# A decoder layer with a routed feed-forward: one flat loop of chunks on TensorE, and one chunk's code in inner loops on ScalarE and VectorE

## What is computed

```python
logits = x @ Wg.T                                     # x: 4096 x 512, normalised rows
top_v, top_i = jax.lax.top_k(logits, 2)
gates = jax.nn.softmax(top_v, axis=-1)
pos = jnp.cumsum(onehot, axis=0) - 1                  # place of a token in its expert's list
keep = pos_f < cap                                    # cap = 1280 rows per expert
exp_batches = zeros((8, cap, 512)).at[flat_e, pos_safe].set(x[tok], mode='drop')
h = jnp.einsum('ecd,edf->ecf', exp_batches, W1)       # 512 -> 2 x 1024
inp, gate = jnp.split(h, 2, axis=-1)
h = jax.nn.gelu(inp, approximate=False) * gate
exp_out = jnp.einsum('eci,eid->ecd', h, W2)           # 1024 -> 512
out = segment_sum(where(keep, gates_f, 0)[:, None] * exp_out[flat_e, pos], tok)
```

## Time and profile before

| | |
|---|---|
| median of three runs | 1554.05 us (1553.39 to 1558.0) |
| profiled execution, its own time | 1552.01 us |
| span of its instructions | 1550.3 us |
| PE busy | 1447.4 us, 93% of the span |
| DVE, ACT, POOL busy | 623.7, 568.7, 366.3 us |
| chain that ended last | PE 81%, DMA 5%, DVE 4%, "issue" 4%, POOL 3%, ACT 2% |
| the experts | from 528.64 us to the end, some 1020 us |

### The profile page before, as it was taken

One profiled execution on the slowest core, in us unless ns is written; L12 is line 12 of the kernel. 1 busy time (PEld: TensorE's weight loads), 2 busy tenths in 40 slices (PEclk: granted clock), 3 DMA queues, 4 the chain that ended last, 5 costly groups with the idle time before them and its releaser, 6 DMA issues.

```text
span 1550.3 us, 20985 instructions
## 1 busy us (share of the span) xinstructions
PE 1447.4 (93%) x7326; PEld 1214.5 (78%) x7327; DVE 623.7 (40%) x1383; ACT 568.7 (37%) x977; POOL 366.3 (24%) x354
## 2 busy tenths in 40 slices
PE   5999999999984499999999899999999999999998
PEld 4867887788772387888888788898789888897886
DVE  5634565467875243411342431215441431215211
ACT  4433433257865233312342531224431422214211
POOL 3201232137665302011112112021112112021011
PEclk9999999999996699999999999999999999999999
DMA  9100221219445426211253432026532342035112
GB/s 198 54 1 28 82 82 55 82 73 219 130 117 173 130 90 163 61 34 20 67 172 54 126 91 41 2 52 184 148 88 54 107 109 41 0 54 149 14 41 27
DMA packets 80537, 132.20 MB, mean 85 GB/s; under 512 B 31940, under 2 KB 32068, under 8 KB 79464
## 3 DMA queue, kind: packets, MB, share of 16 engines
q1 hardware_dynamic: 63816, 97.41, 21.4%
q0 software_dynamic: 16672, 34.16, 11.8%
HBM read 93.64 MB, written 37.91 MB: 85 GB/s over the span
## 4 chain that ended last, share of the span: by engine, by line
PE 81%; DMA 5%; DVE 4%; issue 4%; POOL 3%; ACT 2%; SPq 0%; ACTq 0%; DVEq 0%; POOLq 0%
PE pg L947 16%; PE pg L948 16%; PE pg L949 15%; PE pj L947 8%; PE pj L949 8%; PE pj L948 8%; DMA stage<-w 2%; DMA slot_table<-pack,dest 2%; POOL slot_table L601 2%; PE pt L1301 1%; PE pg L1144 1%; PE pj L1178 1%; DVE w_lo L1364 1%; PE pt L965 1%; DMA out_rows<-ost,etab 1%
## 5 line engine op out<-in xcount | busy, mean ns | idle before, releaser
L947 PE MATMUL pg<-xe_hi,w_hi 128*128 128x512 f32 (+2 forms) x1088 | 393.9, 362 | 22.3 <-DVE w_lo L1364 12.4
L948 PE MATMUL pg<-xe_lo,w_hi 128*128 128x512 f32 (+2 forms) x1088 | 393.0, 361 | 0.0
L949 PE MATMUL pg<-xe_hi,w_lo 128*128 128x512 f32 (+2 forms) x1088 | 392.4, 361 | 0.0
L1755 DVE TENSOR_TENSOR hp<-gl,pg 128x512 f32<-128x512 f32 (+1 forms) x136 | 87.1, 641 | 606.2 <-ACT gl L900 606.2
L678 POOL DMA_INDIRECT out_rows<-ost,etab x62 | 99.8, 1610 | 781.5 <-issue 405.6
L947 PEld LDWEIGHTS pg<-xe_hi,w_hi 128*128 128x128 f32 x1088 | 207.5, 191 | 54.1 <-DVE w_lo L1364 14.4
L900 ACT ACTIVATE gl<-pg 128x512 f32<-128x512 f32 (+1 forms) x136 | 76.1, 560 | 457.2 <-PE pg L949 457.1
L949 PEld LDWEIGHTS pg<-xe_hi,w_lo 128*128 128x128 f32 x1088 | 207.6, 191 | 28.4
L948 PEld LDWEIGHTS pg<-xe_lo,w_hi 128*128 128x128 f32 x1088 | 207.5, 191 | 28.4
L947 PE MATMUL pj<-w_hi,hg_hi 128*128 128x512 f32 x464 | 183.3, 395 | 0.0
L949 PE MATMUL pj<-w_hi,hg_lo 128*128 128x512 f32 x464 | 180.7, 390 | 0.0
(11 more groups left out here) (238 smaller groups left out, 1951.3 us busy)
## 6 DMA issues: line engine op xcount, KB each, us to landing
stage<-w SPq DMA_DIRECT2D x96, 512.0 KB, 4.9
xr<-x SPq DMA_DIRECT2D x8, 1024.0 KB, 8.6
out_rows<-xr SPq DMA_DIRECT2D x8, 1024.0 KB, 7.3
x_rows<-xn SPq DMA_DIRECT2D x8, 1024.0 KB, 6.4
x_in<-x SPq DMA_DIRECT2D x7, 1024.0 KB, 5.2
late_xT<-xT_hi SPq DMA_DIRECT2D x2, 1024.0 KB, 3.9
late_xT<-xT_lo SPq DMA_DIRECT2D x2, 1024.0 KB, 5.9
xT_hi<-late_xT SPq DMA_DIRECT2D x2, 1024.0 KB, 4.7
```

Of the source, the lines that this page charges most:

```text
L947: nc.tensor.matmul(o, lh, rh, start=start, stop=False)
L948: nc.tensor.matmul(o, lh, rl, start=False, stop=False)
L949: return nc.tensor.matmul(o, ll, rh, start=False, stop=stop)
L1755: v.tensor_tensor(hp[j % 2][:, 0:w], gl[j % 2][:, 0:w], pg[:, 2 + j % 2, 0:w], ALU.mult).then_inc(s_hp, 1)
```

## The change

On **TensorE** the two loops become one of 24 turns over all experts' chunks. The registers of the following chunk (expert, chunk, rows left, place of its first tile) are made while the output tiles of the chunk at hand are computed, with one load from `meta` between output tiles 0 and 1. The empty tiles wait for nothing and become 128-column matmuls into `pg`.

On **ScalarE** and **VectorE** the code of one chunk stands once, in a loop over three chunks inside the loop over experts, at full width (512 columns) for every chunk. Four registers are loaded per expert, not three. The W2 pieces of an expert are all split at the head of its first chunk, before the first gelu, and the W1 pieces of the next expert are split in its last chunk, one after each slice.

```diff
         @block.scalar (inside the loop over experts)
-                def jobs(c):
-                    w = CHUNKS[c] * P
-                    act.wait_ge(s_y, tb + 4 * c + 1)
-                    for j in range(FJ + 1):
-                        if j < FJ:
-                            act.wait_ge(s_h, (ib + c) * FJ + j + 1)
-                            if j >= 2:
-                                act.wait_ge(s_hp, (ib + c) * FJ + j - 1)
-                            a.activation(gl[j % 2][:, 0:w], pg[:, j % 2, 0:w], ACT.Gelu).then_inc(s_gl, 1)
-                        if j >= 1:
-                            act.wait_ge(s_hp, (ib + c) * FJ + j)
-                            a.activation(hg_hi[:, j - 1, 0:w], hp[(j - 1) % 2][:, 0:w],
-                                         ACT.Copy).then_inc(s_hghi, 1)
-                        if c == 0 and 2 <= j < 2 + W2P:
-                            split(e, W1P + j - 2)
...
-                        if last:
-                            with act.If(e < EX - 1):
-                                for s in range(i * per, (i + 1) * per):
-                                    split(e + 1, s, ib + c)
...
+                three_chunks = act.value_load(meta[0:1, 3, bass.ds(e, 1)], min_val=0, max_val=1)
+
+                with act.Fori(0, len(CHUNKS)) as c:
+                    left = act.snap(count - c * (4 * P), min_val=-8 * P, max_val=CAP)
...
+                    with act.If(left > 0):
+                        with act.If(c < 1):
+
+                            act.wait_ge(s_y, first + 1)
+                            for s in range(W1P, WP):
+                                split(e, s)
+                        for j in range(FJ + 1):
+                            if j < FJ:
+                                act.wait_ge(s_h, done + (j + 1))
+                                if j >= 2:
+                                    act.wait_ge(s_hp, done + (j - 1))
+                                a.activation(gl[j % 2][:], pg[:, j % 2, :], ACT.Gelu).then_inc(s_gl, 1)
+                            if j >= 1:
+                                if j == 1:
+                                    act.wait_ge(s_y, first + 1)
+                                act.wait_ge(s_hp, done + j)
+                                a.activation(hg_hi[:, j - 1, :], hp[(j - 1) % 2][:], ACT.Copy).then_inc(s_hghi, 1)
+                                with act.If(weights_next > 0):
+
+                                    split(e + 1, j - 1)
+                        evac(range(2))
+                        out_scaled(0)
+                        with act.If(next_is_full > 0):
+                            evac(range(2, 4))
+                        out_scaled(1)
+                        with act.If(c < 2):
+                            out_scaled(2)
+                            out_scaled(3)
         @block.tensor
-            with pe.Fori(0, EX) as e:
-                count = pe.value_load(meta[0:1, 0, bass.ds(e, 1)], min_val=0, max_val=CAP)
-                tb = pe.value_load(meta[0:1, 1, bass.ds(e, 1)], min_val=0, max_val=EX * ET)
-                ib = pe.value_load(meta[0:1, 2, bass.ds(e, 1)], min_val=0, max_val=EX * 3)
-                three_chunks = pe.value_load(meta[0:1, 3, bass.ds(e, 1)], min_val=0, max_val=1)
-
-                with pe.Fori(0, len(CHUNKS)) as c:
...
+            with pe.Fori(0, EX * len(CHUNKS)):
+                with pe.If(pe.snap(at_e, min_val=0, max_val=EX) < EX):
...
+                    out_tile(0)
+                    pe.reg_load(at_next, meta[0:1, 0, bass.ds(e + 1, 1)])
+                    coming = pe.snap(at_next, min_val=0, max_val=CAP)
+                    with pe.If(next_is_full > 0):
+                        turn_next(range(2, 4))
+                    pe.reg_mov(at_left, (left - 4 * P) * more + coming * (more < 1))
+                    pe.reg_mov(at_e, e + (more < 1))
+                    pe.reg_mov(at_c, (c + 1) * more)
+                    pe.reg_mov(at_first, following)
+                    pe.reg_mov(at_done, done + FJ)
+                    out_tile(1)
         @block.vector (inside the same two loops)
+                        with dve.If(c < 1):
+                            for s in range(W1P, WP):
+                                split(e, s)
+                        for j in range(FJ + 1):
...
+                                with dve.If(weights_next > 0):
+                                    split(e + 1, j - 1)
```

More of the change, by code:

```diff
@@ L164, in decoder @@
     etab_next = keep("etab_next", [P, ET, 2], U32)
-    etab = keep("etab", [P, ET, 2], U32)
+    etab = keep("etab", [P, len(CHUNKS) * TI, 2], U32)
     tabinit = keep("tabinit", [P, (EX + 1) * ET, 2], I32)
@@ L924, in outs @@
                         act.wait_ge(s_etc, e + 1)
-                        if c or i >= 2:
-                            act.wait_ge(s_add, 16 * (tb + t))
+                        act.wait_ge(s_add, used if i == 0 else first * 16 + 16 * i)
                         a.activation(ost[i % 2][:], pj[i % 2][:], ACT.Copy,
[L928 to L939, removed]
@@ L940, in _, with evac @@
-                with act.Else():
-                    outs(0, True, CHUNKS[0])
+                                     scale=etab[:, bass.ds(c * 4 + i, 1), 1:2].rearrange("p o w -> p (o w)").bitcast(F32)
+                                     ).then_inc(s_yev, 1)
+                    def evac(tiles):
+                        for i in tiles:
+                            act.wait_ge(s_xet, following + (i + 1))
+                            a.activation(xe_hi[:, :, i * P:(i + 1) * P],
+                                         pt[i % 2][:].rearrange("p (k t) -> p k t", k=KC), ACT.Copy).then_inc(s_xehi, 1)
@@ L1313, in out_tile, with empty_tiles @@
                         ins.then_inc(s_y, 1)
[L1315 to L1340 removed]
+                    def empty_tiles(tiles):
+                        for i in tiles:
+                            mm(pg[:, 0, 0:P], hg_hi[:, 0, 0:P], w2_hi[:, 0, 0:P], start=True,
+                               stop=True).then_inc(s_y, 1)
@@ new lines, in _ @@
+                    with pe.If(left > 3 * P):
+                        up(4)
+                    with pe.Else():
+                        with pe.If(left > 2 * P):
+                            up(3)
+                        with pe.Else():
+                            up(2)
+                    more = pe.snap(left > 4 * P, min_val=0, max_val=1)
+                    next_is_full = pe.snap((c % 2) * more < 1, min_val=0, max_val=1)
+                    gathered = pe.snap((first + (c < 2) * 2) * 16 + next_is_full * 32, min_val=32,
+                                       max_val=16 * (EX * ET + 16))
@@ L1341, in _ @@
+                    pe.reg_mov(at_e, e + (more < 1))
[3 more added lines that the diff above has]
+                    out_tile(1)
+                    with pe.If(c < 2):
+                        with pe.If(left > 2 * P):
+                            out_tile(2)
                             with pe.If(left > 3 * P):
@@ L1343, in _ @@
                             with pe.Else():
-                                empty_tile(3)
+                                empty_tiles(range(3, 4))
+                        with pe.Else():
+                            empty_tiles(range(2, 4))
         @block.vector
```

119 lines of the change are left out of this document (48 added, 71 removed).

## The result

The changed kernel takes 1566.94 us, the median of six runs (1563.59 to 1573.11), and the kernel before 1556.76 us by its six. The ratio is 1.008, with a 95% interval of 1.0049 to 1.011: slower by 0.8%. That is 10.2 us by these medians and 12.5 by the ratio. The forecast was 1566.6.

What follows compares the result with a forecast made beforehand. PE's matmuls plus PE's holes were taken to bound the kernel. 33.0 us come, 28.5 go, the first expert adds 8.1: +12.6 on the profiled 1552.0 gives 1564.6, plus 2.0 for the median 1566.6 us; range 1554 to 1577.

Steps and rivals of the forecast that it cites:

- W2 of this expert: First chunks of the seven experts after the first: pieces before the first gelu hold TensorE's third slice; holes sum to 24.5 us.
- The late copy at e3: Start of the fourth expert: the previous expert's last scaled copy waits for an add on ScalarE, 6.7 us more hole.
- The clock: PE's clock falls after the five holes of 2.6 us and more, 1.7 us each, 8.5 in all.
- e4: Start of the fifth expert, first chunk of three tiles: hole of 3.8 us at PE's third slice, clock fall of 1.7.
- e6: Start of the seventh expert: hole of 3.2 us (1.2 + 0.7 + 1.3) at PE's third slice, clock fall of 1.7.
- e0: First expert's first chunk: late W2 pieces hold the first gelu; hole 7.4 us, clock 2.4, less 1.7 won: +8.1.
- W1 of the next expert: Pieces fit in the last chunk's slices, so w_lo is no longer late at any start: 12.4 us of waits go.
- TensorE's part: Four head loads go; one load and register moves between output tiles cost nothing; the empty tile's 0.6 us wait goes.
- the 28.5 us: All that can be won at the seven later experts' starts: 19.7 idle, 1.3 counting correction, 7.5 clock.
- Same: Path to the first hp 1.2 us shorter, clock falls at only three starts: about 1554 to 1556 us; chance 0.15.
- faster: TensorE's third slice not held at six of seven starts, path 2.5 us shorter at two: about 1543 us; chance 0.10.
- Worse: Table switches cost another 1.28 us each, 1586, or late pieces hold gelus in two-tile last chunks, 1575 to 1579; chance 0.13.

Runs made afterwards that it cites:

- the last version: The changed kernel with W2 pieces behind slice 1, four output buffers, W1 pieces from slice 2 on, two at slice 4: 1529.75 us, 0.9813 of the kernel before.
- four buffers: The changed kernel with four output buffers ost, so scaled copies of tiles 2 and 3 skip the wait for an add: 1552.35 us, 0.9986 of the kernel before.

## Why the prediction was right, and where it was not

**The size and the sign** were right: +12.6 us by the sum, 12.4 in the pair of traces. That the time agrees to 0.4 us is in part luck: by the medians the change costs 10.2 us, and inside the sum the holes came 2 us shorter than forecast and the clock's part 2.5 longer. Two steps behind the sum were wrong in their cause, and they cancel, which is luck too.

**W2 of this expert: right.** The third slice waits for the first hp at every first chunk. The path from the last copy was put at 11.9 us and took 11.5: 3.69 to the table load where I had 4.1, and 7.8 from there. An empty turn of the inner loop, put at 0.7, costs 0.9 at e3 (903.06 - 898.45 - 3.69). The late copy at e3 was put at 6.7 us; it began 6.0 us after the one before it (898.45, and the second of the two behind 891.83, at 892.42). The seven holes sum to 22.5 us against 24.5 forecast.

**The clock: right in kind, small in size.** It fell at the five starts that I named, and cost 11 us where I had 8.5, as I took 1.7 everywhere and e4 and e6 cost 2.8 and 3.0.

**e0: right.** A hole of 7.9 us against 7.4, a fall of the clock of 1.7 against 2.4, and 1.7 won at the head; moving its pieces gave 9.3 back.

**W1 of the next expert: wrong.** The step "so w_lo is no longer late at any start: the 12.4 us go" fails. `w_lo` was late at none. I took the label of a wait at its word, and didn't hold it against rows that I had printed myself. The pieces' place in the slices is worth 30 us and more in the changed kernel, by ScalarE's copies, which the prediction doesn't have at all.

**TensorE's part: wrong.** "I cost this at nothing" holds for what was added between the output tiles: no hole stands there. But the loads that go were given only the starts labelled "issue", and the 28.5 us are theirs: the four loads, with the turns of the loop without a chunk and the waits of empty tiles, held all seven starts. Taken alone this part wins 15 to 19 us and leaves 7.7 us of idle time for hp. In the changed kernel it wins nearly nothing, as the run with ScalarE's and VectorE's part alone shows (1.0054 against 1.008, with intervals that overlap): the time by which PE starts earlier it then waits at the third slice.

That is how a wrong attribution gave the right time. Everything winnable at the starts was counted from PE's idle time, whoever ended it; the new wait was counted from ScalarE's path. For TensorE's part alone the same picture gave 8 to 10 us less, by the expectation for that run, and it was 15 to 19 less.

**The rivals.** *Same* and *faster* needed a path shorter by 1.2 or 2.5 us; it was shorter by 0.4. *Worse* by a price of table switches is out: in the rows of e2 above, the second load starts 0.02 us after the last piece ends (792.75 + 3.90 = 796.65), and gelu 0.02 us after the load. So the load's 1.28 us is the whole price of the second one. The Trainium skill's 1.38 us of drain for a switch to another set (ScalarE: Activation LUTs, What ACT_TABLE_LOAD costs) does not show there; the rows don't name the sets, so whether this load changes the set stays open. Late pieces in two-tile chunks don't show either: PE waits for nothing between the holes.

## What to carry to other kernels

A wait on a counter is labelled with its last increment: before pricing it, look up when the count that the instruction needs was reached. Work that a change moves ahead of an engine's first step in a stage is priced on that stage's critical path, even where the engine is 38% busy, as ScalarE is here; the same work one step later left holes of 2.8 and 1.5 us, and none in the last version, with four buffers and the W1 pieces moved. Two parts of a change that shorten and lengthen the same path don't add: price each with the other in place, and alone.

## What the runs showed of the hardware

Behind an idle time of about 2 us the clock went either way. Behind 2.26 us at e1 it fell to a mean of 0.66 over 5 us in the changed kernel; behind the same 2.26 us at e1, with W2 moved at e0 alone, it stayed at 1.00 (609.24 to 614). Behind 2.01 us it fell and behind 2.48 it didn't, in one trace (four buffers). Over the experts no idle time of up to 1.5 us ended in a fall, leaving out the start of e0, where the clock was at 0.50 already, and each from 2.50 us on did. What decides between was not found.

Code that no kernel here changes took up to 16 us more or less from trace to trace: PE's first matmul of e0, behind 1.50 us of idle time in both, stood at 526.55 us with four buffers and at 542.60 in the last version; in the pair of the result it stood at 528.64 and 535.67. In the changed kernel's trace one such place is an idle time of 2.92 us at 371 us, where the kernel before has 0.54, with the clock at 0.60 over the 5 us behind it.

```profile
370.96 2.91 PE L1144 MATMUL pg<-kv,qT 128*128 128x130 f32 x16 [2.92 <-DVE kf L1560]
```
